# Attention and a mixture of experts on one core: two of four key chunks multiplied as fp16 halves

## The reference, cut to what matters

```
h    = layernorm(x)
q, k, v = h @ Wq, h @ Wk, h @ Wv              # 2 heads of 64
s    = where(adj > 0, (q * 64**-0.5) @ k.T, -9e15)
sat  = softmax(s) @ v                          # both heads side by side
out  = concat(sat[:2048] @ weightr, sat[2048:] @ weightd) + bias
x    = x + leaky_relu(out, 0.01)
h2   = layernorm(x)
gate = h2 @ Wg + bg;  mask = one_hot(top2(gate), 8 experts)
y_e  = gelu(h2 @ W1[e] + b1[e]) @ W2[e] + b2[e]
x    = x + sum over e of mask[:, e] * y_e
```

## Time and profile before

| | us |
|---|---|
| median of 3 runs | 818.61 (818.47 to 819.36) |
| the profiled execution | 818.16 |
| its span | 816.4 |

### The profile page before, as it was taken

How to read it: one execution, slowest core, us unless ns; L and a number is a source line. 1 busy time by engine, 2 the same in 40 slices (tenths; PEclk the granted TensorE clock), 3 DMA queues, 4 the chain that set the end, 5 groups by cost and what they waited for, 6 DMA issues and landing times.

```text
span 816.4 us, 33455 instructions
## 1 busy us (share of the span) xinstructions
PE 786.0 (96%) x12592; PEld 585.1 (72%) x12592; DVE 643.5 (79%) x1469; ACT 684.2 (84%) x1099; POOL 481.1 (59%) x494
## 2 busy tenths in 40 slices
PE   3889999999999999999999999999998999999997
PEld 1357777777777777777777777777777667777775
DVE  6688898888889898888889888898975775555554
ACT  3678898888888898888888888888887989999996
POOL 4157564747465474747556384745635766676664
PEclk9999999999999999999999999999999999999999
DMA  8633533533344344333443443334100000000000
GB/s 226 116 59 61 85 61 63 85 65 58 59 70 71 58 67 75 63 58 60 68 70 60 67 79 58 58 61 80 32 0 2 2 15 15 15 13 13 13 13 14
DMA packets 40909, 45.09 MB, mean 55 GB/s; under 512 B 22168, under 2 KB 32160, under 8 KB 40864
## 3 DMA queue, kind: packets, MB, share of 16 engines
q0 software_dynamic: 9216, 33.56, 25.6%
q1 hardware_dynamic: 31216, 10.71, 5.7%
q10 hardware_dynamic: 432, 0.20, 0.1%
HBM read 71.72 MB, written 2.10 MB: 90 GB/s over the span
## 4 chain that ended last, share of the span: by engine, by line
PE 75%; POOL 11%; issue 6%; DVE 3%; ACT 2%; DMA 1%; POOLq 0%; DVEq 0%; ACTq 0%
PE ps L1045 22%; PE ps L994 20%; PE ps L1015 19%; POOL prob L443 11%; PE ps L1040 6%; PE ps L1057 2%; PE ps L950 1%; PE ps L955 1%; PE ps L965 1%; DVE k_half L811 1%; PE ps L1065 1%; ACT prob L587 1%; PE ps L1168 1%; ACT prob L590 1%; DMA x_sb<-in_x 1%
## 5 line engine op out<-in xcount | busy, mean ns | idle before, releaser
L698 DVE CUSTOM_DVE_ANT_0 prob<-ps,mask 128x1024 f32<-128x1024 f32 x256 | 311.5, 1221 | 36.7 <-PE ps L994 30.7
L512 ACT ACTIVATE prob<-prob,nmax 128x1024 f32<-128x1024 f32 x256 | 293.0, 1144 | 0.0
L1015 PEld LDWEIGHTS ps<-ident,prob 64*128 64x128 f32 x4096 | 152.6, 138 | 61.3 <-issue 58.5
L994 PE MATMUL ps<-k_half,q_row 64*128 64x512 f16 x1536 | 187.6, 376 | 1.9 <-DVE k_half L657 1.5
L1045 PE MATMUL ps<-pt,v_sb 128*64 128x128 f32 x3072 | 188.9, 276 | 0.0
L1015 PE MATMUL ps<-ident,prob 64*128 64x64 f32 x4096 | 180.3, 227 | 4.5 <-ACT prob L512 1.5
L1045 PEld LDWEIGHTS ps<-pt,v_sb 128*64 128x64 f32 x3072 | 165.7, 137 | 6.5 <-issue 0.2
L443 POOL TENSOR_TENSOR prob<-prob 128x512 f16<-128x512 f32 x104 | 123.4, 1189 | 59.3 <-ACT prob L590 56.4
L341 POOL TENSOR_TENSOR pt_lo<-pt_raw,pt_hi 128x1024 f16<-128x1024 f32 x64 | 138.8, 2169 | 5.3
L532 ACT ACTIVATE pt<-ps 128x1024 f32<-128x1024 f32 x96 | 98.3, 1024 | 43.7 <-PE ps L1015 43.4
L338 POOL TENSOR_SCALAR pt_hi<-pt_raw 128x1024 f16<-128x1024 f32 x64 | 79.2, 1237 | 94.2 <-ACT pt_raw L532 79.5
(11 more groups left out here) (118 smaller groups left out, 1075.6 us busy)
## 6 DMA issues: line engine op xcount, KB each, us to landing
mask<-in_adj POOLq DMA_DIRECT2D x64, 512.0 KB, 5.5
q_row<-q_nat SPq DMA_DIRECT2D x128, 32.0 KB, 4.7
x_sb<-in_x SPq DMA_DIRECT2D x4, 512.0 KB, 7.0
out<-x_sb SPq DMA_DIRECT2D x8, 256.0 KB, 2.3
x2t_hi<-in_L_ffn_W SPq DMA_DIRECT2D x1, 1024.0 KB, 6.3
wq_sb<-in_L_gnn_Wq ACTq DMA_DIRECT2D x1, 64.0 KB, 3.0
wk_sb<-in_L_gnn_Wk ACTq DMA_DIRECT2D x1, 64.0 KB, 4.5
wv_sb<-in_L_gnn_Wv ACTq DMA_DIRECT2D x1, 64.0 KB, 5.7
```

What stands on the lines that cost most here:

```text
L512: act.activation(prob[:, h, cols], prob[:, h, cols], ACT.Exp, bias=nmax[:, h:h + 1], scale=-1.0, accum_out=sums[:, j, h, p:p + 1]).then_in ...
L698: dve.tensor_tensor_reduce(out=prob[:, h, col_of(p)], in0=ps[:, 2 * (u % 2):2 * (u % 2) + 2, :].rearrange("p b c -> p (b c)"), in1=mask[:, ...
L994: ins = pe.matmul(ps[:, 2 * (u % 2) + half, :], q_row[part, par, h, a, :], k_half[part, h, b, cols], start=first, stop=final)
L1015: ins = pe.transpose(ps[:, bank + half, t * DH:(t + 1) * DH], prob[part, h, (p * KT + t) * P:(p * KT + t + 1) * P], ident[part, part])
```

## The change

Chunk 3 (units 5 and 7) is split into halves as chunk 1 is, with two buffers `pt_raw` used in turn, so GpSimd makes four splits per row tile in place of two; only the last row tile multiplies chunk 3 as fp32, from `pt_raw`. The halves of the second chunk's values lie over the fp32 values of chunk 1. The layernormed and transposed x of the prologue lies over the halves. GpSimd's step is reordered, with units 5 and 7 split between the weight part, `inverse_std` and `normalise`. Nine weight parts are split in row 0 ahead of the third tile's adjacency load, and the other seven one by one in steps 1, 2, 3, 5, 7, 9 and 11; small weights have a semaphore of their own. The prologue projects the keys of a pair behind the transposes of the next. In the last step of the attention the statistics come at u = 3 and the first operation of the ranking at u = 2, the load of ScalarE's gelu table comes one unit later, and GpSimd makes no split for units 5 and 7. The ranking of the last four row tiles moves from expert 5 of chunk 0 to experts 0 to 7 of chunk 1. `gates_b2` of chunk 0 comes at e = 5. The last `down` makes the products of the high halves of all tiles first, each tile in a bank of its own, and then those of the low halves with a semaphore per tile.

```
-SPLIT_P = 1
-SPLIT_UNITS = (1, 3)
-WHOLE = (0, 2, 4, 5, 6, 7)
+SPLIT_P = (1, 3)
+SPLIT_UNITS = (1, 3, 5, 7)
+NS = len(SPLIT_UNITS)
+WHOLE = (0, 2, 4, 6)
...
+        SMALL_SPLITS, PART_SPLITS, W_PARTS, PARTS_FIRST = 8, 6, 16, 9
...
             def split_pt(j, u, early=False):
...
-                    pool.wait_ge(av_done, NP * j + SPLIT_P - 3)
+                    pool.wait_ge(av_done, NP * j + UNITS[u][1] - 3)
...
-            def step(i, par, prior=True, post=True, load=True, split=True, early=False):
-
-                if prior:
-                    split_pt(i - 1, 1, early)
+            def step(i, par, post=True, load=True, part=None, early=False, last=False):
+
+                split_pt(i - 1, 1, early)
                 if post and par == 0:
                     residual(i - 4)
-                if prior:
-                    split_pt(i - 1, 3, early)
+                split_pt(i - 1, 3, early)
                 if load:
                     load_adj(i + 2, par, 0)
-                if split and par == 0:
-                    split_ffn_part(i)
+                if last:
+                    inverse_std(i - 4)
+                    normalise(i - 4)
+                    return
+                split_pt(i - 1, 5, early)
+                if part is not None:
+                    split_ffn_part(part)
                 if post and par == 0:
                     inverse_std(i - 4)
+                split_pt(i - 1, 7, early)
+                if post and par == 0:
                     normalise(i - 4)
                 if load:
                     load_adj(i + 2, par, 1)
...
-            step(0, 0, prior=False, post=False, split=False)
-            split_values()
             pool.wait_ge(w1_in, 16)
             pool.wait_ge(w2_in, 16)
-            split_ffn_part(0)
+            for n in range(PARTS_FIRST):
+                split_ffn_part(n)
+            load_adj(2, 0, 0)
...
+            load_adj(2, 0, 1)
+            split_values(0)
+            step(1, 1, post=False, part=9, early=True)
+            split_values(1)
+            step(2, 0, post=False, part=10)
+            step(3, 1, part=11)
+            for i in range(4, 12):
+                step(i, i % 2, part=10 + i // 2 if i % 2 else None)
+            pairs(pool, 12, NT - 2, step)
             step(NT - 2, 0, load=False)
             step(NT - 1, 1, load=False)
-            step(NT, 0, load=False, split=False)
+            step(NT, 0, load=False, last=True)
...
-                    to = pt_raw[:, u // 2, :, :]
+                    to = pt_raw[:, u // 2 % 2, :, :]
...
-                project_qk(p)
+                project_q(p)
                 if p < NP - 1:
                     transpose_x(2 * p + 2)
                     transpose_x(2 * p + 3)
+                project_k(p)
...
-                if p == SPLIT_P:
-                    pe.wait_ge(pt_by_pool, 2 * j + 2)
+                if p in SPLIT_P and not whole:
+                    pe.wait_ge(pt_by_pool, NS * j + p + 1)
...
+            def final_down(j, e):
+
+                pe.wait_ge(hid_hi_ready, 16 * j + 2 * e + 2)
+                for t in range(TPC):
+                    rows = slice(t * P, (t + 1) * P)
+                    for b in range(HB):
+                        slot = (2 * e + b) % HID_RING
+                        cols = slice((HB * e + b) * D, (HB * e + b + 1) * D)
+                        for m in range(2):
+                            pe.matmul(ps[:, t, 0:D], hid_hi[:, slot, rows], w2_pair[:, m, cols],
+                                      start=(b == 0 and m == 0), stop=False)
+                pe.wait_ge(hid_lo_ready, lows_by_pool(j, e))
+                pe.wait_ge(hid_lo_by_dve, lows_by_dve(j, e))
+                for t in range(TPC):
+                    rows = slice(t * P, (t + 1) * P)
+                    for b in range(HB):
+                        slot = (2 * e + b) % HID_RING
+                        cols = slice((HB * e + b) * D, (HB * e + b + 1) * D)
+                        ins = pe.matmul(ps[:, t, 0:D], hid_lo[:, slot, rows], w2_pair[:, 0, cols],
+                                        start=False, stop=(b == HB - 1))
+                    ins.then_inc(last_down, 1)
```

More of the change, by code:

```diff
@@ L556, in step @@
                         exp_unit(i, u + EXP_LEAD - NU)
-                    if last and u == 6:
+                    if last and u == 7:
                         act.activation(warm[:, :], expo[:, 0:1], ACT.Gelu)
@@ L679, in _ @@
             normalise_x(5)
[L680 removed]
+            low_k(0)
+            low_q(1)
             shift_x(3)
@@ L795, in keep_logits, with top_gates @@
                                          ALU.add).then_inc(logit_ready, PAIR)
-            def rank_gates(n, first, end):
+            def top_gates(n, first, end):
                 link = linker(gate_chain, GATE_STEPS * n)
-                t_s, count = slice(first, end), end - first
                 dve.wait_ge(logit_ready, end)
@@ L805, in rank_gates, with compare_gates @@
                 link(ins)
+            def compare_gates(n, first, end):
+                t_s, count = slice(first, end), end - first
+                link = linker(gate_chain, GATE_STEPS * n + 1)
                 second = top8[:, t_s, 1:2].to_broadcast([P, count, E])
@@ L808, in rank_gates, with count_above, count_tied @@
                 link(dve.tensor_tensor(tied[:, t_s, :], logit[:, t_s, :], second, ALU.is_equal))
-                link(dve.tensor_reduce(rank[:, t_s, 0:1], above[:, t_s, :], AX_X, ALU.add))
-                for e in range(1, E):
+            def count_above(n, first, end):
+                link = linker(gate_chain, GATE_STEPS * n + 2)
+                link(dve.tensor_reduce(rank[:, first:end, 0:1], above[:, first:end, :], AX_X, ALU.add))
+            def count_tied(n, first, end, experts):
+                t_s = slice(first, end)
+                link = linker(gate_chain, GATE_STEPS * n + 2 + experts[0])
+                for e in experts:
                     link(dve.tensor_tensor(rank[:, t_s, e:e + 1], rank[:, t_s, e - 1:e], tied[:, t_s, e - 1:e], ALU.add))
@@ L845, in step @@
                             leaky(i - 4)
-                        if u == 5:
+                        if u == (3 if last else 5):
                             statistics(i - 4)
+                    if last and u == 2:
+                        top_gates(0, 0, RANKED_EARLY)
                     if last and u == 4:
-                        rank_gates(0, 0, RANKED_EARLY)
+                        compare_gates(0, 0, RANKED_EARLY)
+                        count_above(0, 0, RANKED_EARLY)
+                        count_tied(0, 0, RANKED_EARLY, range(1, E))
             step(0, 0, prior=False, finish=False, post=False)
@@ L907, in combine, with ffn @@
                 ins.then_inc(combined, 1)
-            def ffn(j, par, early=False):
+            def ffn(j, par, early=False, ranking=False, end=False):
                 halve_gates(j)
@@ L914, in ffn @@
                         low_hidden(j, e + 1)
-                    combine(j, e)
+                    combine(j, e, end and e == E - 1)
                     if e == 2:
@@ L923, in ffn @@
                         keep_logits(NT - PAIR, bank=PREP0 + 1)
-                        rank_gates(1, RANKED_EARLY, NT)
-                    if early and e == 6:
+                    if ranking and e == 0:
+                        top_gates(1, RANKED_EARLY, NT)
+                    if ranking and e == 1:
+                        compare_gates(1, RANKED_EARLY, NT)
+                    if ranking and e == 2:
+                        count_above(1, RANKED_EARLY, NT)
+                    if ranking and 2 < e < 6:
+                        count_tied(1, RANKED_EARLY, NT, range(2 * e - 5, 2 * e - 3))
+                    if ranking and e == 6:
+                        count_tied(1, RANKED_EARLY, NT, (7,))
+                    if ranking and e == 7:
                         choose_gates(1, RANKED_EARLY, NT)
             ffn(0, 0, early=True)
-            ffn(1, 1)
-            pairs(dve, 2, NC, ffn)
+            ffn(1, 1, ranking=True)
+            pairs(dve, 2, NC - 2, ffn)
+            ffn(NC - 2, 0)
+            ffn(NC - 1, 1, end=True)
         @block.tensor
@@ L1039, in attend @@
                                 dims = slice(h * DH, (h + 1) * DH)
-                                ins = pe.matmul(ps[dims, AV, 0:P], v_pair[:, values, t, dims], probs[:, h, t, :],
-                                                start=False, stop=False)
+                                ins = pe.matmul(ps[dims, AV, 0:P], v_pair[n][:, values, t, dims],
+                                                probs[:, 2 * n + h, t, :], start=False,
+                                                stop=(tile == NT - 1 and values == 1))
                     else:
@@ L1184, in ffn @@
                         gate_transpose(j)
-                    if e == 4:
+                    if e == (5 if early else 4):
                         gates_b2(j)
```

136 lines of the change are left out of this document (74 added, 62 removed).

## The result

| | us |
|---|---|
| before, median of 4 runs | 818.54 (817.46 to 819.36) |
| changed, median of 4 runs | 826.26 (824.61 to 827.58) |
| ratio | 1.0094, 95% interval 1.0072 to 1.0116 |
| span of the profiled execution, before and changed | 816.4 and 823.7 |

A forecast was written before the change was run, and what follows sets the result against it. TensorE was taken to bound the kernel, with GpSimd given the new work. Terms -13.6 + 10.5 + 4 - 1.1 - 1.5 - 2.0 - 0.8 = -4.5 us took 818.61 to 814.1 us, range 806 to 823.

The forecast's parts named there:

- The step that failed: Attention pairs: ScalarE's 5.3 us and VectorE's 4.3 us free per pair, less 0.88, cover the added waits; cost nothing.
- the third rival: Attention pairs: mask passes sit out splits, VectorE becomes the bound from 1.1 us per pass; 826 us, chance 0.07.
- the second rival: x2_transpose in odd steps: stalls exceed the halves' saving from 1.07 us each; 826 us, chance 0.18.
- x2's wait: Odd steps 5 to 31: TensorE stalls 0.75 us for normalised rows behind unit 7's split, 14 times; +10.5 us.
- The saving: Attention products: second chunk as halves takes 1.46 us instead of 1.90, in 31 row tiles; -13.6 us.
- The first rows: Early row tiles: nine weight parts delay the adjacency load, then GpSimd is full; +4 us, bounds +1 and +8.
- Prologue: Query and key projections: transposes between them shorten a round from 5.6 to about 5.2 us; -1.1 us.
- drain: Last attention step: statistics ahead of the ranking remove x2's transpose wait of 1.48 us; -1.5 us.
- ranking: Feed-forward: seven tiny additions taking 4.86 us in chunk 0 spread over chunk 1; -2.0 us.
- last down: Last combination: high halves first, one bank per tile, first of four starts a good microsecond sooner; -0.8 us.

The follow-up runs named there:

- e5_parts_in_loop: Changed kernel with GpSimd's steps 4 to 11, weight parts included, in a loop instead of written out; 823.69 us (ratio 1.0072).
- e6_all_written_out: Kernel of e1_norm_first with all of GpSimd's attention steps written out, no weight work beyond step 11; 827.69 us (ratio 1.0116).
- e12_larger_op_first: Kernel of e6_all_written_out plus a GpSimd fill of an unused 128x256 tile ahead of each split of unit 1; 811.53 us (ratio 0.992).
- e1_norm_first: Changed kernel with GpSimd's even step making normalise ahead of the split of unit 7 instead of behind it; 815.65 us (ratio 0.9956).
- e4_small_edits: Kernel before with only the changed orders of prologue, last step, ranking and last down; attention and weights as before; 812.79 us (ratio 0.9926).
- e11_small_edits_again: The kernel of e4_small_edits run again; 812.46 us (ratio 0.9932).
- e10: Changed kernel, normalise first, GpSimd's steps looped, seven weight parts ahead of third adjacency load, none in steps 1 to 3, nine in odd steps 5 to 21; 807.79 us.

## Why the prediction was wrong

**The step that failed** is that the time free on ScalarE and VectorE covers whatever meets them ("of which 0.88 goes; I cost both at nothing"), for the pairs with a weight part, together with the claim against the third rival that "in even steps the first mask pass comes before the copy that GpSimd waits for". For unit 1's copy the trace of the kernel before already says otherwise. ScalarE's copy ends at 324.69, the mask pass comes 0.24 us behind that end, and it is first at the port only because GpSimd starts 0.10 us later still:

```profile
323.66 1.03 ACT L532 ACTIVATE pt_raw<-ps 128x1024 f32<-128x1024 f32 x1 [0.23 <-PE ps L1015]
324.93 0.69 DVE L664 TENSOR_SCALAR mask<-mask 128x2048 bf16<-128x2048 bf16 x1
325.03 1.49 POOL L338 TENSOR_SCALAR pt_hi<-pt_raw 128x1024 f16<-128x1024 f32 x1 [2.53 <-ACT pt_raw L532]
```

That is a loop. In steps 4 to 11 the change writes GpSimd's steps out, and the order turns: in step 6 the split is first by 0.05 us, in steps 8 and 10 the mask pass falls into GpSimd's DMA issue and ends behind the split's first operation. e5_parts_in_loop shows 1.2 to 1.3 us for each of these three pairs (38.05 to 38.5 us), and e6_all_written_out and e12_larger_op_first show the same price for the meeting of step 6. The weight part adds about 0.5 us in each of four pairs. The prediction had -0.5 us for these four pairs (4 x (0.75 - 0.88)), the trace has +6.95. The rival with this mechanism got 0.07; it named VectorE's waits as the price and the right rule, but wanted them in all pairs. That it and the second rival both name 826 us, the time that was measured, is chance: neither has its condition met, 1.1 us for each mask pass or 1.07 us for each stall.

**x2's wait** was the right mechanism with a term too small. 0.75 us a pair was predicted; moving normalise gave back 0.92 (e1_norm_first). Over 14 stalls that is 2.4 us.

**The saving.** 0.88 us a pair was taken. With nothing else in the way the pair is 35.38 us, 0.73 below 36.11 (e1_norm_first). TensorE's rows show the 0.88 us in the products (1.46 us for a chunk of halves and 1.90 for a whole one, as before), but the scores of the pair take 10.71 us in place of 10.64. The rest of the missing 0.15 us is open; TensorE is busy in all but 0.09 us of that pair.

**The first rows.** +4 was predicted. Step 5's x2 is at 128.74 against 124.4 in e4_small_edits and 122.70 in e11_small_edits_again, 4.3 to 6.0 us later (this point differs by 1.7 us between executions of one kernel). By then the halves have saved some 1.3 us and the first stall of 0.87 us is in it, so the term itself is 4.8 to 6.5 us, in the range of 1 to 8. e10 shows that the two causes named were right as a pair: with fewer parts ahead of the load and none in steps 1 to 3 it is at 124.09. They weren't run apart.

**Prologue, drain, ranking, last down.** -5.4 predicted, -5.5 and -5.9 measured as a whole; the single terms were not run apart. The traces of e4_small_edits and the kernel before, laid side by side, say that the sum is right in part by luck. The first scores start 2.2 us sooner (3.3 in e11_small_edits_again), where the prologue's term was -1.1. The stretch from step 31 to the transpose in the last step is 1.54 us shorter (-1.5 predicted). From there to the last chunk's first combination it is 1.58 us (-2.0, the ranking), and from that to the end of the last combination 0.92 us (-0.8). But what follows the last combination takes 3.74 us in place of 2.90, in every kernel with these edits, so the new last `down` gains next to nothing; the cause is open. Two of these can be seen in the changed kernel too: x2's transposes in the last step no longer wait, where the earlier trace rows had 1.48 us:

```profile
635.87 0.44 PE L1131 MATMUL ps<-ident,x 128*128 128x128 f32 x2
```

and the query projections follow each other after 4.65 us (21.48, 26.13) in place of 5.61, where the prediction had 5.2.

**The sum against the measurement.** Forecast -4.5, measured +7.7. Of the 12.2 us between them, 7.4 are the four pairs with parts: 3.6 for the written-out code (by e5_parts_in_loop), 2.4 for the parts, and 1.4 for x2's longer wait and the smaller saving. These last two make another 2.5 us in the nine pairs behind. The remaining 2.3 us lie ahead of step 5 and behind step 31.

## What to carry to other kernels

Where VectorE's pass and GpSimd's operation take the same port, ask of each meeting who is first and by how much: a lead of 0.1 us read from a trace is no cover, and any edit near it, even one that only turns a loop into written-out code, can reverse it. When an engine off the critical path gets twice the work, its average is not the question; look for the short operations that a busy engine waits for and put them ahead of the long new ones. Run the small edits of a large change by themselves: here they gained 5.5 us and hid that the main part lost 13.5.

## What the runs showed of the hardware that was not expected

GpSimd starts a split 0.19 us behind the copy it waits for in written-out code (e6_all_written_out) and 0.35 us behind it in a loop (e1_norm_first); no run shows why. The mask pass at 185.42 was issued while GpSimd was issuing a DMA (185.12 to 185.72) and waited through it and through the next operation, which started at 185.75; whether the DMA issue holds the port was not tried. A 128x256 fill on GpSimd (0.31 us) ahead of each split of unit 1 made the kernel 16 us faster. The fill was under way (325.67 to 325.98) when the mask pass started at 325.85, and the pass took its 0.69 us all the same.

The Trainium skill ("SBUF — State Buffer", section "SBUF: two separate sides") has whoever starts first hold the shared port pair for its whole instruction. The meetings of a mask pass and a split agree with it: the pass takes 0.69 us where it starts first and 1.54 where it starts 0.05 us behind, and the leaky relu behind it 1.26 and 2.35 us. The pass at 185.42 doesn't by itself: it started 0.33 us ahead of the split and waited for it.
